# A fused attention and MLP block: the loop over head pairs written out, the es transposes moved ahead of the weight pairs

## The reference

```
q, k = rope(xn @ Wq.T), rope(xn @ Wk.T)          # 16 heads of 128
v, g = xn @ Wv.T, xn @ Wg.T
s    = clip(xn @ Ws1.T @ Ws2.T + bs2, -32, 32)   # 64 slots a head
es, enz = exp(s), exp(-cumlogsumexp(s, tokens))
A    = tril(q @ k.T * scale)
ok   = enz * (A @ es)
p    = softmax(ok)
W2   = tril((p * enz) @ es.T)
o    = W2 @ v
attn = (rmsnorm(o) * g_norm * silu(g)) @ Wo.T
mlp  = (gelu(xn @ Wgate.T) * (xn @ Wup.T)) @ Wdown.T   # weights are 4-bit codes with scales
```

## Time and profile before

| what | value |
|---|---|
| median of three runs | 1187.22 us (1184.56 to 1188.18) |
| the profiled execution | 1186.13 us, its span 1184.4 us |
| mean granted TensorE clock | 0.986 |
| TensorE busy | 1114.7 us, 94% |
| VectorE busy | 943.1 us, 80% |
| ScalarE busy | 642.1 us, 54% |
| GpSimd busy | 419.6 us, 35% |
| DMA | 23.19 MB, mean 20 GB/s |

### The profile page before, as it was taken

How to read it: one execution, slowest core, us unless ns; L and a number is a source line. 1 busy time by engine, 2 the same in 40 slices (tenths; PEclk the granted TensorE clock), 3 DMA queues, 4 the chain that set the end, 5 groups by cost and what they waited for, 6 DMA issues and landing times.

```text
span 1184.4 us, 20879 instructions
## 1 busy us (share of the span) xinstructions
PE 1114.7 (94%) x6872; PEld 941.6 (79%) x6872; DVE 943.1 (80%) x1808; ACT 642.1 (54%) x1748; POOL 419.6 (35%) x306
## 2 busy tenths in 40 slices
PE   6789999999999998999989999899998999999995
PEld 5568888888788887888878888788887888788884
DVE  6888887888868887888877888778886888877763
ACT  5355564655645565555655556464563565655451
POOL 5233242433513335232443324343251433523231
PEclk9899999999999999999999999999999999999998
DMA  4001000100001000010000100001000100000001
GB/s 157 1 1 74 1 1 1 52 22 1 1 2 73 1 1 2 1 73 1 1 3 1 74 1 1 3 16 59 1 1 2 73 1 1 1 2 19 1 19 36
DMA packets 9117, 23.19 MB, mean 20 GB/s; under 512 B 816, under 2 KB 5808, under 8 KB 7984
## 3 DMA queue, kind: packets, MB, share of 16 engines
q1 hardware_dynamic: 9008, 21.76, 5.0%
HBM read 19.66 MB, written 2.10 MB: 18 GB/s over the span
## 4 chain that ended last, share of the span: by engine, by line
PE 71%; issue 8%; DVE 6%; ACT 6%; POOL 3%; POOLq 0%; DVEq 0%; ACTq 0%
PE bank L203 17%; PE bank L205 16%; PE bank L204 16%; PE bank L292 5%; ACT xs L568 3%; PE bank L305 3%; PE bank L349 2%; DVE xs L860 2%; POOL qkT L1087 2%; PE bank L294 2%; DVE Wt L740 2%; ACT xs L567 2%; PE bank L282 1%; PE bank L338 1%; PE bank L341 1%
## 5 line engine op out<-in xcount | busy, mean ns | idle before, releaser
L1096 POOL TENSOR_TENSOR inter_lo<-ffb,inter_hi 128x512 fp32r<-128x512 f32 x64 | 83.3, 1323 | 433.2 <-ACT inter_hi L617 433.2
L1087 POOL TENSOR_TENSOR qkT<-ra,xs 128x512 f32<-128x512 f32 x128 | 163.5, 1277 | 95.1 <-DVE xs L860 67.6
L586 ACT ACTIVATE sm<-bank,mx 128x64 f32<-128x64 f32 x256 | 76.3, 325 | 168.5 <-DVE mx L816 168.5
L857 DVE TENSOR_TENSOR ra<-bank,rope 128x512 f32<-128x512 f32 x128 | 88.0, 687 | 55.1 <-ACT xs L568 54.9
L805 DVE RECIPROCAL enzT<-enzT 128x256 f32<-128x256 f32 x64 | 111.6, 1744 | 0.0
L860 DVE TENSOR_TENSOR xs<-xs,rope 128x512 f32<-128x512 f32 x128 | 109.0, 852 | 0.0
L203 PE MATMUL bank<-xh,wqk_hi 128*128 128x512 f32 x256 | 107.4, 420 | 0.0
L203 PE MATMUL bank<-xh,wgu_hi 128*128 128x512 f32 x256 | 106.9, 418 | 0.0
L591 ACT ACTIVATE At<-bank 128x128 f32<-128x128 f32 x128 | 35.4, 276 | 132.0 <-DVE At L740 132.0
L205 PE MATMUL bank<-xh,wgu_lo 128*128 128x512 f32 x256 | 101.6, 397 | 0.0
L203 PE MATMUL bank<-wvg_hi,xh 128*128 128x512 f32 x256 | 101.4, 396 | 0.0
(11 more groups left out here) (137 smaller groups left out, 3211.5 us busy)
## 6 DMA issues: line engine op xcount, KB each, us to landing
raw<-in_w_qkvg SPq DMA_DIRECT2D x8, 1024.0 KB, 4.9
scaled<-in_w_scaled SPq DMA_DIRECT2D x8, 640.0 KB, 7.7
packed<-in_w_packed SPq DMA_DIRECT2D x8, 384.0 KB, 5.4
acc<-in_x SPq DMA_DIRECT2D x4, 512.0 KB, 8.6
out<-acc SPq DMA_DIRECT2D x4, 512.0 KB, 3.0
ws_raw<-in_w_slot SPq DMA_DIRECT2D x8, 48.0 KB, 1.8
rope<-in_rope_tab SPq DMA_DIRECT2D x1, 256.0 KB, 7.0
osq<-in_w_slot SPq DMA_DIRECT2D x1, 128.0 KB, 3.3
```

Source lines behind the costliest of these rows:

```text
L857: dve.tensor_tensor(two(ra[i % 2][:, :]), two(pj[i][:, :]), cos, ALU.mult).then_inc(cos_done, 1)
L1087: pool.tensor_tensor(qkT[:, i, :], ra[i % 2][:, :], xs[i % 2][:, :], ALU.add).then_inc(roped, 1)
L1096: pool.tensor_tensor(inter[1][e][:, :], ffb[e][:, :], inter[0][e][:, :].bitcast(F32), ALU.subtract).then_inc(inter_lo, 1)
```

## The change

Four things are changed together. (1) `each_stage` and the loop of SyncE are written out in full, so semaphore values are constants. (2) The sc banks no longer alternate: score and weight blocks take sc[i % 2], slot scores sc[0], ok rows sc[1]. (3) The es transposes go to rg[1], between the read of the transposed p by slot_query and weight pair 0; copy_J moves on ScalarE to before the copies of weight blocks 0 and 1, and values(1) waits for it. (4) q/k tile 3 moves behind weight pair 1, and on VectorE diagonals 2 and 3 go ahead of rope 2; on ScalarE swap 3 goes behind the copies of blocks 2 and 3. Score blocks 0 and 1 of a stage wait for the weight block that last used their own bank.

The core of the diff (the rest drops the bp and kind arguments of the helpers):

```diff
--- before.py
+++ after.py
@@ -185,18 +183,11 @@
             return slice(bp * TOK, (bp + 1) * TOK) if tile is None else slice(
                 bp * TOK + tile * P, bp * TOK + (tile + 1) * P)
 
-        def sc_bank(bp, kind, i=0):
-            return sc[(SC_STEP * bp + SC_SLOTS[kind][i]) % 2]
-
         def each_stage(eng, stage):
 
-            for bp in range(BP):
-                stage(0, bp, bp == 0, False)
-            with eng.Fori(1, HP - 1) as hp:
+            for hp in range(HP):
                 for bp in range(BP):
-                    stage(hp, bp, False, False)
-            for bp in range(BP):
-                stage(HP - 1, bp, False, bp == BP - 1)
+                    stage(hp, bp, hp == bp == 0, hp == HP - 1 and bp == BP - 1)
 
         def three(pe, dst, stat, mov, start, stop):
@@ -319,7 +310,7 @@
             def slot_weights(st, bp, b):
 
                 t0 = b * T
-                pair = [(sc_bank(bp, "W", 2 * b + h), slice(h * M, (h + 1) * M)) for h in range(2)]
+                pair = [(sc[h], slice(h * M, (h + 1) * M)) for h in range(2)]
                 for dst, g in pair:
                     pe.matmul(dst[:, 0:T], esT[bp % 2][g, t0:t0 + P], qe[g, t0:t0 + T], start=True, stop=True)
                 for dst, g in pair:
@@ -425,12 +416,10 @@
 
 
                 for i in (0, 1):
-                    if first and i == 1:
-                        pe.wait_ge(clip_done, 1)
-                    elif first or i == 1:
-                        pe.wait_ge(J_ready, st + 1)
+                    if first:
+                        pe.wait_ge(clip_done if i == 1 else J_ready, 1)
                     else:
-                        pe.wait_ge(W_off, 4 * st)
+                        pe.wait_ge(W_off, 4 * st - 1 + i)
                     scores(st, bp, i, hp)
                 mlp_up(st, bp, hp, 0)
                 mlp_up(st, bp, hp, 1)
@@ -478,31 +467,30 @@
                     project_qk(st + 1, nbp, nhp, 0)
                     project_qk(st + 1, nbp, nhp, 1)
                 pe.wait_ge(qe_ready, st + 1)
-                pe.wait_ge(A_off, 4 * st + 4)
-                if not last:
+                if not last:
+                    pe.wait_ge(es_ready, st + 2)
+                    slot_transpose(rg[1], esT[nbp % 2])
                     pe.wait_ge(clip_done, st + 2)
                 slot_weights(st, bp, 0)
                 if not last:
                     project_qk(st + 1, nbp, nhp, 2)
                 if first:
                     transpose_x(3)
-                if not last:
-                    project_qk(st + 1, nbp, nhp, 3)
                 pe.wait_ge(W_off, 4 * st + 2)
                 slot_weights(st, bp, 1)
+                if not last:
+                    project_qk(st + 1, nbp, nhp, 3)
                 pe.wait_ge(v_ready, 4 * st + 4)
                 if first:
                     slot_inner(3, rg[1])
                 else:
                     pe.wait_ge(acc_done, 2 * st)
                 values(st, bp, 0)
-                if not last:
-                    pe.wait_ge(es_ready, st + 2)
-                    pe.wait_ge(W_off, 4 * st + 3)
-                    slot_transpose(sc_bank(bp, "E", 0), esT[nbp % 2])
                 if first:
                     pe.wait_ge(h1_done, 8)
                     pe.wait_ge(h1_lo, 4)
+                elif not last:
+                    pe.wait_ge(J_ready, st + 2)
                 values(st, bp, 1)
 
             each_stage(pe, stage)
@@ -700,24 +688,24 @@
                 if not last:
                     swap_halves(st + 1, 0)
                     swap_halves(st + 1, 1)
+                    copy_J(st + 1, rg[1][:, :])
                 off_diagonal(*w_args, 0, 1.0)
                 off_diagonal(*w_args, 1, 1.0)
                 if bp == 3 and more:
                     split_hi(hp + 1, W_GU)
                 if bp == 2 and more:
                     split_slot(hp + 1)
+                if not last:
+                    swap_halves(st + 1, 2)
                 if first:
                     x_hi(3)
-                if not last:
-                    swap_halves(st + 1, 2)
-                    swap_halves(st + 1, 3)
                 off_diagonal(*w_args, 2, 1.0)
                 off_diagonal(*w_args, 3, 1.0)
+                if not last:
+                    swap_halves(st + 1, 3)
                 if first:
                     inner_copy(3, rg[1])
                 square_o(st, 0)
-                if not last:
-                    copy_J(st + 1, sc_bank(bp, "E", 0)[:, :])
                 square_o(st, 1)
 
             each_stage(act, stage)
@@ -1021,12 +1009,11 @@
                     rope_sin(st + 1, 1)
                 if first:
                     x_lo(3)
+                diagonal(*w_args, 2, mask_w, (o_full, 2 * st))
+                diagonal(*w_args, 3, mask_w, (o_full, 2 * st))
                 if not last:
                     rope_cos(st + 1, 2)
                     rope_sin(st + 1, 2)
-                diagonal(*w_args, 2, mask_w, (o_full, 2 * st))
-                diagonal(*w_args, 3, mask_w, (o_full, 2 * st))
-                if not last:
                     rope_cos(st + 1, 3)
                     rope_sin(st + 1, 3)
                 if first:
```

More of the change, by code:

```diff
@@ L56 @@
 W_VG, W_QK, W_GU, W_OD = range(4)
-SC_SLOTS = {"A": (0, 1, 2, 3), "S": (4,), "K": (5,), "W": (6, 7, 8, 9), "E": (10,)}
-SC_STEP = 11
 def build(nc, x, w_qkvg, w_packed, w_scaled, w_slot, w_slot1, g_norm, rope_tab, out):
@@ L223, in _ @@
                     sp.dma_start(scaled[:, :], w_scaled[0]).then_inc(scaled_in, 16)
-            with sp.Fori(0, HP - 1) as hp:
+            for hp in range(HP - 1):
                 sp.wait_ge(w_lo, 4 * hp + 4)
@@ L276, in slot_scores @@
                     pe.wait_ge(ws2_lo, 4 * hp + 4)
-                pe.matmul(sc_bank((bp - 1) % BP, "S")[:, :] if n is not None else sc[1][:, :],
+                pe.matmul(sc[0][:, :] if n is not None else sc[1][:, :],
                           ws2[:, :], h1[:, bp, :], start=True, stop=True).then_inc(S_full, 1)
@@ L289, in scores @@
                     pe.wait_ge(roped, 4 * st + 2 * h + 2)
-                dst = sc_bank(bp, "A", i)
+                dst = sc[b]
                 t0 = b * T
@@ L309, in slot_reads, with slot_rows @@
                 mm.then_inc(ok_full, 1)
-            def slot_rows(st, bp):
+            def slot_rows(st):
                 pe.wait_ge(okz_done, st + 1)
-                dst = sc_bank(bp, "K")
+                dst = sc[1]
                 for i in range(NT):
@@ L387, in transpose_x @@
                     if bp == 3 and k == 1:
-                        pe.wait_ge(qe_ready, 1)
+                        pe.wait_ge(J_ready, 2)
                     for i in range(NT):
@@ L462, in stage @@
                     project_vg(st + 1, nbp, nhp, 2, True)
-                slot_rows(st, bp)
+                slot_rows(st)
                 if not first:
@@ L488, in stage @@
                     transpose_x(3)
+                pe.wait_ge(W_off, 4 * st + 2)
+                slot_weights(st, bp, 1)
                 if not last:
                     project_qk(st + 1, nbp, nhp, 3)
-                pe.wait_ge(W_off, 4 * st + 2)
-                slot_weights(st, bp, 1)
                 pe.wait_ge(v_ready, 4 * st + 4)
@@ L577, in copy_J, with softmax_exp @@
                 act.activation(esJ[:, :, :].rearrange("p n m -> p (n m)"), src, ACT.Copy).then_inc(J_ready, 1)
-            def softmax_exp(st, bp):
+            def softmax_exp(st):
                 act.wait_ge(mx_done, st + 1)
@@ L582, in softmax_exp @@
                 wait(act, rs_done, st)
-                src = sc_bank(bp, "K")
+                src = sc[1]
                 for g in range(8):
@@ L587, in softmax_exp, with off_diagonal @@
                 ins.then_inc(p_ready, 1)
-            def off_diagonal(diag, done, dst, bp, kind, st, i, scale):
+            def off_diagonal(diag, done, dst, st, i, scale):
                 act.wait_ge(diag, 4 * st + i + 1)
-                act.activation(dst[i][:, 1, :], sc_bank(bp, kind, i)[:, P:2 * P], ACT.Copy,
+                act.activation(dst[i][:, 1, :], sc[i % 2][:, P:2 * P], ACT.Copy,
                                scale=scale).then_inc(done, 1)
@@ L662, in stage @@
                 npar = (bp + 1) % 2
-                a_args = (A_diag, A_off, At, bp, "A", st)
-                w_args = (W_diag, W_off, Wt, bp, "W", st)
-                more = not (isinstance(hp, int) and hp == HP - 1)
+                a_args = (A_diag, A_off, At, st)
+                w_args = (W_diag, W_off, Wt, st)
+                more = hp < HP - 1
                 off_diagonal(*a_args, 0, SCALE)
@@ L693, in stage @@
                     prepare_out(hp + 1)
-                softmax_exp(st, bp)
+                softmax_exp(st)
                 if not last:
@@ L734, in two, with diagonal @@
                 return ap.rearrange("p (b t) -> p b t", b=2)
-            def diagonal(full, done, dst, bp, kind, st, i, mask, used):
```

(17 more changed lines are left out.)

## The result

The changed kernel takes 1156.96 us (median of four runs, 1156.18 to 1157.61) against 1187.70 for the kernel before on the same chip: ratio 0.9745, 95% interval 0.9724 to 0.9765. The prediction was 1148 with a range of 1142 to 1160. So the direction and the range held, but the time lies outside the forecast's own range of 1144 to 1152: some 9 us of the expected 38 did not come.

The account below looks back on a forecast made before the run. TensorE was taken as the bound, with stalls, jumps and lower clock to remove. Gains 26.0 - 4.7 + 12.1 + 4.5 = 37.9 us off the profiled 1186.13 gave 1148.2, forecast as 1148, range 1142 to 1160.

Parts of the forecast that it names:

- Term (a): At stage ends, moved es transposes and VectorE's diagonals ahead of rope 2 remove TensorE's stalls: 26.0 us gained.
- (c): At the loop's five jumps back, writing the loop out removes the idle time at no new price: 12.1 us gained.
- (d): TensorE's lower clock after waits of over 2 us goes when those waits go: 4.5 us gained.
- The replay of the border: Stage ends bp=2 and bp=3 recomputed from trace rows: no wait at pair 1 (0.3 us to spare at bp=2) or values(1).
- What has little room: Gated transposes behind bp=1 and bp=2, where decode follows rope 3: 0.85 us of room shrinks to 0.2.
- rival 1: New waits at weight pair 1 and the gated transposes give part back: 1159 us; chance 0.18.
- Term (b): One tile behind each weight pair adds changes between kinds of matmul on TensorE: 4.7 us lost, 0 to 6.5.
- Rival 4: Changes of kind on TensorE cost nothing extra, so the gain is larger: 1143 us; chance 0.07.
- Rival 2: Idle time at the jumps comes with the stage group and stays in straight code: 1163 us; chance 0.09.
- rival 3: Written-out code stalls on instruction fetches in every stage, ending slower: 1222 us; chance 0.03.
- Term (e): Registers for waits, A_off before the pairs, bank parities and stage 0: no effect; stage 0 within 1 us either way.

Follow-up runs that it names:

- Experiment 6: Changed kernel with VectorE's old order, diagonals 2 and 3 behind rope 2: 1194.92 us, 1.0067 of the kernel before.
- experiment 3: Changed kernel with GpSimd making only 16 of 1024 columns of the gate/up weights' low part in head pairs 1 to 7: 1150.74 us.
- experiment 7: Changed kernel with decode steps 1 and 3 moved ahead of softmax_max a stage later, and sum_squares(0) ahead of rope 3 with bp=3: 1148.34 us.
- experiment 1: Kernel before with only the loops written out, nothing reordered: 1182.92 us, ratio 0.9963.
- experiment 2: Changed kernel with the whole reordering but the loops kept: 1160.96 us, 0.9795 of the kernel before.
- experiment 9: Kernel of experiment 7 with the loops kept in all engines: 1157.04 us, 0.9747 of the kernel before.
- Experiment 8: Kernel of experiment 7, with GpSimd's v/g split waiting for the first normalisation and stage 0's tile 3 back ahead of pair 1: 1146.43 us.
- 4: Changed kernel with GpSimd's first v/g split put behind its second power: 1158.59 us, 0.9770 of the kernel before.
- 5: Changed kernel with q/k tile 3 put back ahead of weight pair 1: 1180.6 us, 0.9948 of the kernel before.
- 10: Changed kernel with the loop kept in SyncE's program alone: 1157.16 us, 0.9753 of the kernel before.

## Why the prediction was right or wrong

**Term (a), the stalls, 26.0: right in mechanism, and incomplete.** Stalls, jumps and lower clock ((a), (c), (d)) were 42.6 in the prediction; the trace of before has 42.8 above the floor of 33.72 a stage. The replay of the border held: pair 1 behind one tile, its diagonals at once, no wait at the pairs or the values; bp=3 stages fell from 35.98 to 33.96. Experiment 6 shows what would have come of the move without VectorE's new order.

**The step that failed stands in (a) and in "What has little room".** For bp=3 the prediction saw that the split still holds rope_sin of tile 2, and followed only one consequence, tile 3's rotation for scores(2) of the next stage, "there too about 1.2 us are left". That held: scores(2) do not wait. But VectorE works in order, and sum_squares(0) stands behind both ropes. The way over osq, square_o and sum_squares(1) to the gated product was followed for bp=1 and bp=2 and not for this border. It makes the transposes 0.65 late in the bp=0 stages (0.94 in one), 5.3 us, shown by experiment 3. At the other two, where 0.2 us of room was expected, they are 0.14 and 0.18 late and the stages 0.2 longer (3.3 us, shown by experiment 7). The prediction let rope 3 end 0.25 before the next stage starts (571.35 against 571.6); with bp=2 it ends 0.04 behind the start:

```profile
560.82 0.68 DVE L848 TENSOR_TENSOR xs<-xs,rope 128x512 f32<-128x512 f32 x1
561.42 0.68 DVE L733 TENSOR_REDUCE ms<-osq 128x4 f32<-128x512 f32 x1
562.01 1.30 DVE L865 TENSOR_SCALAR codes<-codes 128x768 int32<-128x768 int32 x1
```

That is the second place of rival 1; its first, the weight pairs, did not come. Of the 1159 that rival 1 gave, the gated transposes' part was 4.5 and measured 8.6.

**Term (b), 4.7: mis-sized, it measured 0.** A bp=1 stage without waits takes 33.73, the floor before was 33.72. By the starts of TensorE's instructions in a bp=1 stage, splitting the two tiles costs 0.12 (1.59 and 1.50 against 2.97), near the 0.15 said, and the es transposes 0.06 more at their new place; but values that run through uninterrupted give 0.10 back, and the first two tiles, which no longer run into a weight pair, 0.09. Rival 4 held that the net is nothing, and that came; its reason, that changes of kind cost nothing, did not, and its time did not come because of the waits.

**Terms (c) and (d), 12.1 + 4.5: right in the sum, wrong as separate terms.** (c) took 12.1 for the jumps, but the idle time at the five is 9.7, 0.8 to 2.5 each; the shortest stands behind the lower clock of the stage at 290.11 (38.50, clock 0.96), which (d) did not count. And (d) let every lower clock go with its wait, though only two of the seven waits had been followed by one. Written out alone, the loop gave 4 us (experiment 1): the 2.1 us waits that remained then brought the lower clock in all seven bp=3 stages, some 5, and start and end lost another 5. On top of the reordering it gave 4 again (experiment 2 against after), in part because the jumps had hidden late gated products; with those gone it gave 8.7 (experiment 7 against 9). Rival 2, that idle time stays in straight-line code, is refuted, and so is rival 3: no stall without a cause appears in stages 1 to 31 (the 1.6 us of stage 0 is there with the loops kept as well).

**Term (e), the start, 0 with bounds of 1: wrong by 3.8.** The first matmul is 2.35 late and stage 0 loses 1.4 more; the weights' landing against the normalisation was not in the prediction at all. Experiment 8, which has both edits at once, starts stage 1 at 84.12 and so takes back 1.8 of it. What makes stage 0 itself longer was not isolated. The last 1.4 us are stage 31's: from 18.7 to 24.2 us into it the granted clock is 0.82, and in experiment 7 1.00, in a stage with the same work and the same waits:

```profile
1124.50:1130.00 5.50, 3.35 (x21) 2.48 (x21) 2.38 (x7) 1.40 (x4) 2.50 (x2) 0.82 0.30 98
```

```profile
1116.50:1122.00 5.50, 3.35 (x29) 2.71 (x29) 2.92 (x8) 1.82 (x6) 2.49 (x2) 1.00 0.28 98
```

Kernels with the longer end (49.4 to 50.5: after, experiments 1, 4, 5, 6, 9, 10) and with the shorter (48.0 to 48.3: before, 2, 3, 7, 8) are found with and without loops, so writing out is not the cause; why the clock falls earlier in some of them stays open.

In one sum: 1148.2 predicted for the profiled execution, minus 4.7 for (b), plus 8.6 of new waits, plus 3.8 and 1.4 at the ends is 1157.3; it took 1157.08.

## What to carry to other kernels

When one engine stalls others, follow every instruction queued behind the held one, not only the one whose consumer you were looking at: here the rotation had room, and a reduction two places further back did not. Prices of stalls, jumps and the lower clock do not add up part by part: a jump can hide a wait and a wait can bring a lower clock, so the worth of writing a loop out was 4 us before the stalls were gone and 9 after. And look at the border again after a large gain: moving two decode steps and one reduction on VectorE was worth 8.6 us more.

## What the runs showed that was not expected

- A wait of 2.03 to 2.3 us on TensorE was followed by a lower granted clock (0.78 in the next stage's first 4.08 us in one of them) in all seven bp=3 stages of experiment 1, in three of seven in experiment 6 and in two of seven in the kernel before. The jumps of experiment 9, 1.65 to 1.93 us of idle, brought it once in five times (0.66). What decides it stays open.
- A jump back made its stage 2.2 to 2.7 us longer in the kernel before (0.8 to 2.5 of it idle), where another wait of 2.1 came some 4 us ahead of it, and 1.7 to 2.1 in the reordered ones; the trace gave it once as "issue" and once as a wait for qkT.
- The first DMAs' data come into use at other times in written-out code: x 0.5 us later, the v/g weights 1.6 us earlier. Four fp32 tensor_scalar instructions that met a GpSimd tensor_tensor then took 3.81 us instead of 1.78.
